# Second cross-attention of a fused perceiver kernel: row sums of the exponentials by GpSimd and VectorE instead of ScalarE's accumulator

## The reference, cut to what matters

```python
def _L1_xattn_ref(query, key, value):          # query 16x64x512, key = value = ctx 16x512x512
    Q = query.reshape(B, Sq, H, D).transpose(0, 2, 1, 3)       # H = 16 heads, D = 32
    K = key.reshape(B, Skv, H, D).transpose(0, 2, 1, 3)
    V = value.reshape(B, Skv, H, D).transpose(0, 2, 1, 3)
    scores = jnp.einsum('bhqd,bhkd->bhqk', Q, K) / jnp.sqrt(jnp.asarray(D, Q.dtype))
    weights = jax.nn.softmax(scores, axis=-1)
    out = jnp.einsum('bhqk,bhkd->bhqd', weights, V)
    return out.transpose(0, 2, 1, 3).reshape(B, Sq, E)
x = x + _L1_xattn_ref(_layernorm(x, axis=-1), ctx_1024, ctx_1024)
```

## Time and profile before

| | |
|---|---|
| median of 3 runs | 1468.76 us (1467.66 to 1468.98) |
| the profiled execution's own time | 1466.26 us |
| its span, first to last instruction | 1464.4 us, 32483 instructions |
| busy over the span | PE 93%, PEld 64%, VectorE 74%, ScalarE 40%, GpSimd 10% |
| the second attention | from 1057.0 to 1229.2 us of the span, 172.2 us |
| mean granted TensorE clock | 0.981 |

### The profile page before, as it was taken

One profiled execution on the slowest core, in us unless ns is written; L12 is line 12 of the kernel. 1 busy time (PEld: TensorE's weight loads), 2 busy tenths in 40 slices (PEclk: granted clock), 3 DMA queues, 4 the chain that ended last, 5 costly groups with the idle time before them and its releaser, 6 DMA issues. The chain is left out here.

```text
span 1464.4 us, 32483 instructions
## 1 busy us (share of the span) xinstructions
PE 1364.0 (93%) x13794; PEld 940.7 (64%) x13794; DVE 1083.9 (74%) x2221; ACT 587.7 (40%) x1234; POOL 149.3 (10%) x106
## 2 busy tenths in 40 slices
PE   9999999999999997999988889999799898888898
PEld 5677777777777775435565767667466555677443
DVE  5477777778778787773677699787577786765887
ACT  2344444444444433212223511111388885034543
POOL 3200000000000000230000000100000003154800
PEclk9999999999999999899989999999999999989999
DMA  7343344334443333400006000000355464000000
GB/s 263 105 138 100 119 126 130 113 120 142 152 162 125 113 93 119 149 1 1 3 3 240 28 1 1 0 1 1 119 203 229 178 208 158 35 3 2 8 23 29
DMA packets 50330, 136.88 MB, mean 93 GB/s; under 512 B 10974, under 2 KB 15838, under 8 KB 44043
## 3 DMA queue, kind: packets, MB, share of 16 engines
q1 hardware_dynamic: 50186, 134.82, 27.2%
HBM read 117.73 MB, written 17.07 MB: 92 GB/s over the span
## 5 line engine op out<-in xcount | busy, mean ns | idle before, releaser
L735 ACT ACTIVATE l0x_prob<-l0x_prob,l0x_negmax 128x512 f32<-128x512 f32 x128 | 90.9, 712 | 177.5 <-DVE l0x_negmax L802 177.5
L593 PE MATMUL bank<-l0x_ctxT,l0x_upper_k 128*128 128x512 f32 x256 | 106.8, 417 | 1.3 <-PEq L271 1.3
L606 PE MATMUL bank<-l0x_upper_v,l0x_ctxT 128*128 128x512 f32 x256 | 104.7, 409 | 0.0
L608 PE MATMUL bank<-l0x_upper_v,l0x_ctxT_lower 128*128 128x512 f32 x256 | 101.0, 394 | 0.0
L595 PE MATMUL bank<-l0x_ctxT,l0x_lower_k 128*128 128x512 f32 x256 | 100.8, 394 | 0.0
L607 PE MATMUL bank<-l0x_lower_v,l0x_ctxT 128*128 128x512 f32 x256 | 100.7, 393 | 0.0
L594 PE MATMUL bank<-l0x_ctxT_lower,l0x_upper_k 128*128 128x512 f32 x256 | 100.5, 392 | 0.0
L1071 PE MATMUL bank<-ident,l1x_prob 128*128 128x128 f32 x512 | 78.9, 288 | 13.2 <-ACT l1x_prob L1141 9.2
L1141 ACT ACTIVATE l1x_prob<-l1x_prob,l1x_negmax 128x512 f32<-128x512 f32 x128 | 91.0, 715 | 0.0
L1190 DVE CUSTOM_DVE_ANT_0 l1x_prob<-bank,l1x_zeros 128x512 f32<-128x512 f32 x128 | 80.8, 687 | 13.8 <-PE bank L1056 13.8
L1071 PEld LDWEIGHTS bank<-ident,l1x_prob 128*128 128x128 f32 x512 | 55.6, 143 | 51.0 <-ACT l1x_prob L1141 41.2
(11 more groups left out here) (346 smaller groups left out, 3125.6 us busy)
## 6 DMA issues: line engine op xcount, KB each, us to landing
l0x_whole<-in_turned_context SPq DMA_DIRECT2D x16, 1024.0 KB, 5.4
l1x_KT<-in_turned_context SPq DMA_DIRECT2D x16, 1024.0 KB, 7.0
l1x_ctx<-in_ctx SPq DMA_DIRECT2D x16, 1024.0 KB, 4.8
fp_weight<-l0x_weight_piece SPq DMA_DIRECT2D x24, 352.0 KB, 4.8
f_raw<-fp_weight SPq DMA_DIRECT2D x3, 2816.0 KB, 18.6
l0x_abs_piece<-in_L_ffn_w_gate SPq DMA_DIRECT2D x16, 512.0 KB, 4.4
l0x_abs_piece<-in_L_ffn_w_up SPq DMA_DIRECT2D x16, 512.0 KB, 5.4
l0x_abs_piece<-in_L_ffn_w_down SPq DMA_DIRECT2D x16, 512.0 KB, 4.5
```

Source lines behind the costliest of these rows:

```text
L593: nc.tensor.matmul(bank[:, :], w.upper_k[:, kc, cols], c, start=kc == 0, stop=False)
L606: nc.tensor.matmul(bank[:, :], c, w.upper_v[:, kc, :], start=kc == 0, stop=False)
L608: last = nc.tensor.matmul(bank[:, :], c_lower, w.upper_v[:, kc, :], start=False, stop=kc == CH - 1)
L735: nc.scalar.activation(w.prob[r][:, :], w.prob[r][:, :], ACT.Exp, scale=-1.0, bias=w.negmax[:, p:p + 1], accum_out=w.rowsum[:, b % 2, p:p ...
```

## The change

ScalarE's exponentials lose their `accum_out`. GpSimd gets a `fold(k)` for every quad: from the four probability tiles together (now one tensor `probs`, of which the old tiles are views), it adds the upper half of the keys to the lower (4 x 256 results a partition), then halves that to 4 x 128 and to 4 x 64 in one of two `tail` tiles. VectorE gets a `row_sums(k)`, one reduction of a `tail` tile to four sums, run two quads later and before `finish_heads`. New waits: GpSimd's first fold waits for the quad's fourth exponential; each further fold waits for the one before it; VectorE's `scored_max(k)` waits for the first fold of quad k - 2; `row_sums(k)` waits for the third fold of quad k; `finish_heads` waits for the row sums instead of the exponentials. The eight adds to X are put between the folds: tile t = 0 to 6 behind the fold of quad 4t + 6, the last behind all. The new buffers lie in space that was free in this stage.

```diff
--- before.py
+++ after.py
@@ gpsimd
-            for t in range(TILES):
+
+            def fold(k):
+
+                p, part, tail = w.probs[:, 4 * (k % 2):4 * (k % 2) + 4, :], w.part, w.tail[k % 2]
+                pool.wait_ge(exp_done, 4 * k + 4)
+                if k > 0:
+                    pool.wait_ge(tail_ready, k)
+                nc.gpsimd.tensor_tensor(part[:, :, :], p[:, :, 0:256], p[:, :, 256:512], ALU.add).then_inc(folded, 1)
+                pool.wait_ge(folded, 2 * k + 1)
+                nc.gpsimd.tensor_tensor(part[:, :, 0:P], part[:, :, 0:P], part[:, :, P:256], ALU.add).then_inc(folded, 1)
+                pool.wait_ge(folded, 2 * k + 2)
+                if k > 1:
+                    pool.wait_ge(row_summed, k - 1)
+                nc.gpsimd.tensor_tensor(tail[:, :, :], part[:, :, 0:64], part[:, :, 64:P], ALU.add).then_inc(tail_ready, 1)
+
+            def add_heads(t):
+
                 pool.wait_ge(heads_done, 2 * t + 2)
                 nc.gpsimd.tensor_tensor(g.X[:, t, :], g.X[:, t, :], w.heads[t % 2][:, :], ALU.add).then_inc(x_done, 1)
+
+            for k in range(QUADS):
+                fold(k)
+                if k % 4 == 2 and k > 4:
+                    add_heads((k - 6) // 4)
+            add_heads(TILES - 1)
@@ scalar
-                b, p = k // 2, 4 * (k % 2) + r
+                p = 4 * (k % 2) + r
                 act.wait_ge(scored, 4 * k + r + 1)
-                nc.scalar.activation(prob(k, r)[:, :], prob(k, r)[:, :], ACT.Exp, scale=-1.0, bias=w.negmax[:, p:p + 1],
-                                     accum_out=w.rowsum[:, b % 4, p:p + 1]).then_inc(exp_done, 1)
+                nc.scalar.activation(prob(k, r)[:, :], prob(k, r)[:, :], ACT.Exp, scale=-1.0,
+                                     bias=w.negmax[:, p:p + 1]).then_inc(exp_done, 1)
@@ vector
             def scored_max(k):
 
                 dve.wait_ge(score_full, k + 1)
+                if k > 1:
+                    dve.wait_ge(folded, 2 * (k - 2) + 1)
...
+            def row_sums(k):
+
+                b, p = k // 2, 4 * (k % 2)
+                dve.wait_ge(tail_ready, k + 1)
+                nc.vector.tensor_reduce(w.rowsum[:, b % 4, p:p + 4], w.tail[k % 2][:, :, :], AX.X, ALU.add).then_inc(row_summed, 1)
+
             def finish_heads(b):
 
                 t, tokens = b // 2, slice(b % 2 * T, (b % 2 + 1) * T)
-                dve.wait_ge(exp_done, (b + 1) * PAIRS)
+                dve.wait_ge(row_summed, 2 * b + 2)
...
             for k in range(QUADS):
                 if k > 0:
                     turned_copy(k - 1, 3)
+                if k > 1:
+                    row_sums(k - 2)
                 if k % 2 == 1 and k > 1:
                     finish_heads(k // 2 - 1)
...
             early_variances()
             turned_copy(QUADS - 1, 3)
+            row_sums(QUADS - 2)
+            row_sums(QUADS - 1)
             finish_heads(B - 1)
@@ buffers
+        w.part = a("l1x_part", [P, 4, 256], F32)
+        w.tail = [a(f"l1x_tail{i}", [P, 4, 64], F32) for i in range(2)]
...
-        w.prob = [a(f"l1x_prob{i}", [P, KEYS], F32) for i in range(8)]
+        w.probs = a("l1x_probs", [P, 8, KEYS], F32)
+        w.prob = [w.probs[:, i, :] for i in range(8)]
```

More of the change, by code:

```diff
@@ L1004, in cross_attention @@
     scalar_copied, vector_copied = s_("scalar_copied"), s_("vector_copied")
+    folded, tail_ready, row_summed = s_("folded"), s_("tail_ready"), s_("row_summed")
     half_full, heads_out, heads_back = s_("half_full"), s_("heads_out"), s_("heads_back")
```

## The result

The changed kernel takes 1471.53 us (median of 10 runs, 1467.42 to 1473.67); the kernel before, run beside it, 1467.70 us. The ratio is 1.0026, interval 1.0015 to 1.0037: slower by 3.8 us, between 2.2 and 5.4. The forecast was 1470.3, in a range of 1464 to 1478, with "no measurable change" as the likeliest case.

The account below looks back on a forecast made before the run. It took PE to set the pace before and GpSimd after the change; the last fold at 1224.5 plus a 5.15 us tail ended the stage 1.4 us later, so 1468.8 + 1.4 = about 1470.3 us, range 1464 to 1478.

Parts of the forecast that it names:

- no measurable change: Whole kernel: a result within 2.9 us (0.2%) of none, given a chance of 0.43.
- GpSimd becomes the pace-maker: Second attention loop: GpSimd needs 4.93 us a quad, above the others' 4.45 and below the present average of 5.06.
- The sum 157.7 us for folds and adds: GpSimd in the loop: 32 quads of folds at 4.63 us plus seven adds to X at 1.36.
- rival 2: GpSimd's chain of folds is longer than thought, deciding from 4.68 us a quad; at 4.85, +8 us, 1477; 27%.
- Rival 1: GpSimd's folds run faster than flat adds, at 3.8 us a quad; net -2.4 to -5.2 us, 1463.6 to 1466.4; 24%.
- ScalarE's exponentials start 0.1 us closer, and a quad falls from 4.61 to about 4.45: ScalarE without accumulator readouts: 13 us off ScalarE; 4.45 us is the joint pace of PE, ScalarE and VectorE.
- VectorE's sums cost nothing in the loop: VectorE's reductions, 0.7 us a pair, are mostly hidden by 0.61 us of waits; without such room, 11 us.
- No lock for L1190: VectorE's L1190 stays at 0.687 us beside GpSimd; the rival, that it takes the lock, gives about 1520, 3%.
- The 13.6 us of stalls are then covered by the lag: PE's stalls in 30 quads are covered by GpSimd's lag, leaving one further loss of about 0.3 us.
- The tail: +1.4 against 1228.26: Stage end: last fold at 1224.5 plus 5.15 us exposed gives 1229.7 against 1228.3, so +1.4 us.
- The change touches none of the stalls: PE in the loop: 13.6 us above 30 x 4.61, where PE waits for nothing shown, stay untouched.
- The pace of 4.61: PE in plain quads sets 4.61 us a quad; ScalarE's exponentials hold it up by at most 0.15 to 0.25.

Follow-up runs that it names:

- e4: Changed kernel with one more small GpSimd add (4 x 16 elements) in every fold; 1477.63 us, ratio 1.0069 to the kernel before.
- e7: Changed kernel without the 25 transfers of 1 MB that reload keys and contexts in the loop; 1468.77 us, ratio 1.0003 to the kernel before.
- e10: Changed kernel with each reload of keys or contexts cut into four transfers, issued spread out; 1468.66 us, ratio 1.0005 to the kernel before.
- e6: Second attention without row sums (a constant instead) and without the 25 reload transfers of 1 MB; 1449.64 us, ratio 0.9870 to the kernel before.
- e8: Kernel before, with only quad 31 folded on GpSimd and summed on VectorE; 1474.49 us, ratio 1.0040 to the kernel before.
- e12: Changed kernel with early_variances moved behind VectorE's copy of the last transposed tile; 1471.59 us, ratio 1.0020 to the kernel before.
- e2: Second attention without row sums: no accumulator, folds or VectorE sums, a constant instead; reloads kept; 1467.05 us, ratio 0.9991 to the kernel before.
- e3: Changed kernel with every fourth quad and the last two summed by ScalarE instead of folded; 1468.28 us, ratio 0.9996 to the kernel before.
- e5: Kernel before without the 25 transfers of 1 MB that reload keys and contexts in the loop; 1454.11 us, ratio 0.9904 to the kernel before.
- e9: Kernel before with each reload of keys or contexts cut into four transfers, issued spread out; 1455.96 us, ratio 0.9926 to the kernel before.

## Why the prediction was right and where it was wrong

- **GpSimd becomes the pace-maker: right.** The sum 157.7 us for folds and adds came to 32 x 4.70 + 7 x 1.04 = 157.7 (a quad cost 0.07 more, an add 0.3 less). That these two cancel to 0.1 us is luck; at 4.70 a quad without the cheaper adds the sum would have passed 2.9 us, as rival 2 says from 4.68 up. e4, e7 and e10 show that the chain binds. Rival 1, folds at the rate of L2467, is out: 2.378 us for 1024 elements is the flat add.
- **ScalarE's exponentials start 0.1 us closer, and a quad falls from 4.61 to about 4.45: right.** 0.61 and 4.43 were measured.
- **VectorE's sums cost nothing in the loop: right**, since 4.43 and 4.42 (e6, without the sums) are the same to 0.01 us.
- **No lock for L1190: right.** The 0.687 us stood. VectorE was held elsewhere, where I had not looked: at the TENSOR_SCALAR of `early_variances`, which had run beside an idle GpSimd. The Trainium skill, SBUF — State Buffer, section "SBUF: two separate sides", names VectorE instructions in a two-port mode among those that the lock holds; the six rows that end with the fold agree with it (no row shows the mode that they ran in), and the reductions from SBUF, 0.41 us beside the folds, are not held.
- **"The 13.6 us of stalls are then covered by the lag": the size was off.** Besides the 1.9 us before quad 1 the forecast had 0.3 us of idle GpSimd; it was 0.30 and 0.97 beyond the usual gap of 0.14, about 1.3. Relative to the start of the stage the last fold ended 0.5 us later than forecast (the first one came 0.2 earlier there).
- **The tail: +1.4 against 1228.26 was mis-sized, by little.** The 5.15 us behind the last fold came to 5.09. But the sum followed the last add to X alone. It did not price what stands behind VectorE's delayed `early_variances` on PE: a product that waits 3.7 us, a granted clock at 0.50, transposes in 3.0 us. Then ScalarE's copies and not the add end the stage, 0.2 us behind it (0.7 in e8, 0.8 in e12). The stage grew by 2.1 us in the profile, of which the forecast had 1.4, the late last fold is 0.5 and the copies 0.2.
- **The rest of the 3.8 us has no cause shown.** It is not in this stage: in the two profiles 0.5 us lies ahead of it and 1.1 behind it, in parts that the change does not touch and that scatter by more than that (from the last add to the end of the span it is 236.1 us before, 237.4 after, and 235.4 to 241.4 in the other profiles). The interval of the difference begins at 2.2 us.
- **"The change touches none of the stalls": wrong, and it did not show in the total.** With quads at 4.42 PE's pauses grew from 8.9 to 11.9 us (e2), and the stalls as a whole from 13.6 to 19.6. Had GpSimd been free, as in rival 1, its -2.4 to -5.2 us would hardly have come: e3 with room on GpSimd gave -0.6 (-3.2 to +2.1). The pace of 4.61 was not what the loop's length hung on; the reloads were.

That PE waits in these pauses for blocks of its own instructions is shown by their places and by the packets that end them; that the pauses go with the reloads is shown by e5 and e9. That the instruction packets stand behind the reloads in the DMA engines is the reading that joins the two: the trace does not show when a packet was asked for.

## What to carry to other kernels

A pause of the bounding engine that nothing in the program releases is a term of its own: find what it goes with (here reloads of 1 MB in one transfer, in the same DMA engines as PE's instructions) before freeing another engine, since freed time can flow into it. Work moved to a slow engine is cheap only under cover, so ask at both ends of a loop what is left exposed: here the last two quads held the whole loss, and leaving them with ScalarE took it back. And an engine that was idle until now can hold out its neighbour: look for short instructions elsewhere in its time that shared something with it.

## What the runs showed of the hardware beyond expectation

- Cutting reloads of 1 MB into four and issuing them evenly took 10.9 us (0.0074 of the ratio) off a kernel in which no instruction waited for these loads.
- PE's instructions came in packets of 16 KB, one for about 124 matmuls with their weight loads, and all 73 pauses of PE without a releaser in these loops ended 1.19 to 1.68 us behind the end of such a packet.
- A four-element TENSOR_SCALAR of VectorE waited out the rest of a GpSimd add in six of six profiles (0.57 to 2.16 us instead of 0.17), while custom instructions (0.687) and copies (0.684) that read PSUM and a reduction (0.410) that read SBUF did not.
- Behind PE's waits at the end of the stage (3.70 us in the profile after; 1.59, 0.49 and 0.87 in e8; 2.96, 0.49 and 2.47 in e12) its granted clock was 0.50, its lower level of 1.2 GHz, and 16 transposes took 3.0 to 3.7 us instead of 1.9.
